# Convolution of the short channel chunk on GpSimd for two of four batches, and all stores of projection parts on SyncE's queue

## What is computed

```python
# mixer: depthwise convolution over time (7 taps), pointwise step, ReLU, pairwise maximum, 2-D DFT
h = conv_general_dilated(h, w_dw, padding='SAME', feature_group_count=192) + b_dw
h = einsum('od,bds->bos', w_pw, h) + b_pw
h = reduce_window(relu(h), -inf, max, (1, 1, 2), (1, 1, 2), 'VALID')
y = real(fft2(transpose(h)));  h = layernorm(y) * gamma + beta
# linear attention with a Taylor feature map, 12 heads of 16, causal
h = h + attention(layernorm(h))
# mixture of 8 experts, one per token, plus features of a tridiagonal resolvent
h = h + ffn(layernorm(h))
```

## Time and profile before

| what | value |
|---|---|
| timed runs | 428.26, 429.86, 433.29 us; median 429.86 |
| profiled execution | 426.79 us, its span 425.0 us |
| mean granted TensorE clock | 0.933 of full |
| TensorE matmul busy | 379.0 us, 89% of the span |
| VectorE busy | 281.1 us, 66% |
| ScalarE busy | 160.5 us, 38% |
| GpSimd busy | 103.0 us, 24% |
| DMA | 47.94 MB, mean 113 GB/s |

### The profile page before, as it was taken

One profiled execution on the slowest core, in us unless ns is written; L12 is line 12 of the kernel. 1 busy time (PEld: TensorE's weight loads), 2 busy tenths in 40 slices (PEclk: granted clock), 3 DMA queues, 4 the chain that ended last, 5 costly groups with the idle time before them and its releaser, 6 DMA issues.

```text
span 425.0 us, 7812 instructions
## 1 busy us (share of the span) xinstructions
PE 379.0 (89%) x2658; PEld 255.4 (60%) x2659; DVE 281.1 (66%) x901; ACT 160.5 (38%) x321; POOL 103.0 (24%) x154
## 2 busy tenths in 40 slices
PE   8999899799998998989998899995899999997273
PEld 4476547133673364723677228894899999996252
DVE  4589734899688995986433853664446656657783
ACT  1001131595317843187531781471243443441000
POOL 2000030151303612045300260310543443421000
PEclk9999899699999999999995799997899999999656
DMA  8664049400685015810279705310411112112504
GB/s 266 194 197 149 0 123 258 126 3 2 191 217 149 2 38 155 217 52 2 68 209 291 333 20 202 129 35 9 164 43 56 45 53 56 43 40 54 169 1 148
DMA packets 26900, 47.94 MB, mean 113 GB/s; under 512 B 11044, under 2 KB 21860, under 8 KB 25332
## 3 DMA queue, kind: packets, MB, share of 16 engines
q1 hardware_dynamic: 21412, 32.73, 25.0%
q10 hardware_dynamic: 2288, 7.15, 6.4%
q0 software_dynamic: 3168, 7.65, 6.2%
HBM read 36.84 MB, written 10.68 MB: 112 GB/s over the span
## 4 chain that ended last, share of the span: by engine, by line
PE 57%; DVE 24%; DMA 6%; issue 5%; ACT 4%; POOL 2%; DVEq 1%; SPq 0%; ACTq 0%; POOLq 0%
PE att L1664 10%; PE ring L1650 8%; PE ring L1654 5%; PE att L1527 4%; PE ring L1515 4%; ACT probs L674 3%; DMA w1b<-q_parts 3%; DVE wide L824 2%; PE att L1490 2%; POOL probs L603 2%; PE att L1581 2%; PE ring L1395 1%; PE ring L1361 1%; DVE stats L833 1%; PE ring L1400 1%
## 5 line engine op out<-in xcount | busy, mean ns | idle before, releaser
L674 ACT ACTIVATE probs<-ring,ones 128x1024 f32<-128x1024 f32 (+2 forms) x72 | 66.3, 970 | 15.9 <-PE ring L1515 14.5
L603 POOL TENSOR_SCALAR_AFFINE_SELECT probs<-probs 128x256 f32<-128x256 f32 (+1 forms) x72 | 40.7, 569 | 111.6 <-ACT probs L674 111.4
L1664 PE MATMUL att<-w,probs 128*128 x276 | 50.6, 335 | 3.3 <-DVE probs L1148 3.3
L1664 PEld LDWEIGHTS att<-w,probs 128*128 128x128 f32 x276 | 45.8, 195 | 4.2 <-issue 4.1
L1515 PE MATMUL ring<-w1b 128*128 128x512 bf16 (+3 forms) x192 | 40.6, 324 | 6.5 <-ACT probs L674 3.6
L824 DVE SCALAR_TENSOR_TENSOR wide<-w,wdw,wide 128x512 f32<-128x512 f32 x60 | 44.1, 779 | 0.8
L1527 PE MATMUL att<-probs,va 128*32 128x512 f32 (+3 forms) x384 | 39.8, 454 | 2.4 <-POOL probs L603 1.8
L629 POOL DMA_INDIRECT ffn_by_token<-probs,target_i x23 | 23.1, 1002 | 52.6 <-DVE probs L1154 44.7
L1515 PEld LDWEIGHTS ring<-w1b 128*128 128x128 bf16 x192 | 13.1, 101 | 37.8 <-ACT probs L674 26.5
L774 ACT ACTIVATE probs<-ring,q_area 128x128 f32<-128x128 f32 x72 | 19.9, 375 | 38.1 <-DVE k_area L1127 13.5
L619 POOL DMA_INDIRECT probs<-x_by_token,source_i x23 | 22.6, 984 | 41.4 <-issue 16.7
(11 more groups left out here) (369 smaller groups left out, 713.7 us busy)
## 6 DMA issues: line engine op xcount, KB each, us to landing
w1b<-k_parts ACTq DMA_DIRECT2D x16, 384.0 KB, 9.8
w1b<-q_parts SPq DMA_DIRECT2D x16, 384.0 KB, 9.1
w<-in_w SPq DMA_DIRECT2D x1, 4608.0 KB
w1a<-in_w1a SPq DMA_DIRECT2D x1, 3072.0 KB, 10.3
w<-in_x SPq DMA_DIRECT2D x4, 512.0 KB, 3.5
w<-in_x SPq DMA_DIRECT2D x8, 256.0 KB, 5.0
q_parts<-q_area SPq DMA_DIRECT2D x12, 128.0 KB, 2.6
k_parts<-k_area POOLq DMA_DIRECT2D x12, 128.0 KB, 2.6
```

What stands on the lines that cost most here:

```text
L603: nc.gpsimd.affine_select(diag, diag, [[0, len(UNITS[n][1])], [1, P]], ALU.is_ge, minus_one, base=0, channel_multiplier=-1).then_inc(p_rea ...
L674: nc.scalar.activation(squares(n), bank[:, :, 0:N - P * j], ACT.Square, bias=ones[:, 0:1], scale=0.25).then_inc(sq_done, 1)
L1664: last = nc.tensor.matmul(att[2][:, 0:D], hT[slot][:, c, :], w2[:, bass.ds((e * HC + c) * D, D)], start=(c == 0), stop=(c == HC - 1))
```

## The change

For the third and fourth batch GpSimd computes `conv_s`. The chain has one instruction for the first tap and two for each of the others, a multiply into a scratch tensor (`short_terms`, two of them in turn, in a free part of w2) and an addition, each waiting for the one ahead (`short_tap`). It stands in GpSimd's `project(b)`, between the selects of two attentions. `pointwise(2)` and `pointwise(3)` wait for it (`short_conv_done`) ahead of the short chunk's matmul, and SyncE's load of the fourth batch's input waits for the third's. VectorE's chain for the short chunk is taken out. GpSimd's stores go to SyncE, which now issues twelve a batch, each part as it is ready.

```diff
@@ -157,6 +157,8 @@
         at += 4 * P
         even_s, odd_s = (w2[:, at + P * i:at + P * i + P] for i in range(2))
         at += 2 * P
+        short_terms = [w2[:, at + N * i:at + N * i + N] for i in range(2)]
+        at += 2 * N
         assert at <= E * HC * D
 
         def of_parity(ap, h):
@@ -345,6 +347,7 @@
 
         zeroed, idle_zeroed = sem("buffers_zeroed"), sem("idle_operand_zeroed")
         conv_done = sem("conv_done")
+        short_tap, short_conv_done = sem("short_tap_done"), sem("short_conv_done")
         taps_ready, tap_sums_done, tap_sums_copied = sem("taps_ready"), sem("tap_sums_done"), sem("tap_sums_copied")
         pw_done = sem("pointwise_done")
         pool_done = sem("pooled_done")
@@ -457,17 +460,6 @@
                 src = dram_[0:2].rearrange("i d h n -> d i (h n)")
             eng.dma_start(dst.rearrange("p h n -> p (h n)"), src).then_inc(s_stack, 16)
 
-        def store_parts(eng, b, h, parts, ready):
-
-            if b > 0:
-                eng.wait_ge(s_stack, 16 * STACK_LOADS * b)
-            for i in range(PARTS):
-                rows = part_dram[h][i].rearrange("d h n -> (d h) n")
-                eng.wait_ge(ready[i], b + 1)
-                eng.dma_start(rows[0:P, :], parts[i]).then_inc(s_part_out[h], 16)
-                eng.wait_ge((s1_ready, s2_ready, s3_ready)[i], b + 1)
-                eng.dma_start(rows[P:D, :], s_parts[i][rows_of(h), :]).then_inc(s_part_out[h], 16)
-
         def store_out(eng, odd):
 
             for i in range(2):
@@ -486,6 +478,8 @@
                 if b > 0:
                     sp.wait_ge(tap_sums_done, min(b, 2))
                     sp.wait_ge(conv_done, 2 * b)
+                    if b > 2:
+                        sp.wait_ge(short_conv_done, b - 2)
                 sp.dma_start(xin[:, 0, HALO:HALO + S], t["x"][b, 0:P, :]).then_inc(s_x, 16)
                 for h in range(2):
                     first = HALO - 2 * h
@@ -504,7 +498,17 @@
 
             def project(b):
 
-                store_parts(sp, b, 0, q_parts, (q1_ready, q2_ready, q3_ready))
+                if b > 0:
+                    sp.wait_ge(s_stack, 16 * STACK_LOADS * b)
+                for i in range(PARTS):
+                    rows = [d[i].rearrange("d h n -> (d h) n") for d in part_dram]
+                    sp.wait_ge((q1_ready, q2_ready, q3_ready)[i], b + 1)
+                    sp.dma_start(rows[0][0:P, :], q_parts[i]).then_inc(s_part_out[0], 16)
+                    sp.wait_ge((k1_ready, k2_ready, k3_ready)[i], b + 1)
+                    sp.dma_start(rows[1][0:P, :], k_parts[i]).then_inc(s_part_out[1], 16)
+                    sp.wait_ge((s1_ready, s2_ready, s3_ready)[i], b + 1)
+                    for h in range(2):
+                        sp.dma_start(rows[h][P:D, :], s_parts[i][rows_of(h), :]).then_inc(s_part_out[h], 16)
                 sp.wait_ge(s_part_out[0], 16 * 2 * PARTS * (b + 1))
                 if b > 0:
                     sp.wait_ge(s_done, NU * b)
@@ -586,8 +590,28 @@
             def front(b):
                 pass
 
+            taps_of = Steps(pool, short_tap)
+
+            def convolve_short(b):
+
+                pool.wait_ge(s_x, 48 * (b + 1))
+                pool.wait_ge(pw_done, 2 * b)
+                for tap in range(TAPS):
+                    src = of_parity(xin[:, 1, tap:tap + S], 0)
+                    w = wdw[:, 1, tap:tap + 1]
+                    if tap == 0:
+                        taps_of.then(nc.gpsimd.tensor_scalar(in_pairs(conv_s), src, w, vec2[:, 0, 1:2], ALU.mult, ALU.add))
+                        continue
+                    term = in_pairs(short_terms[tap % 2])
+                    taps_of.then(nc.gpsimd.tensor_scalar(term, src, w, None, ALU.mult))
+                    last = nc.gpsimd.tensor_tensor(in_pairs(conv_s), in_pairs(conv_s), term, ALU.add)
+                    if tap < TAPS - 1:
+                        taps_of.then(last)
+                last.then_inc(short_conv_done, 1)
+
             def project(b):
-                store_parts(pool, b, 1, k_parts, (k1_ready, k2_ready, k3_ready))
+                if 0 < b < B - 1:
+                    convolve_short(b + 1)
 
             def attend(b):
                 if b == B - 1:
@@ -810,8 +834,6 @@
                     dve.wait_ge(pw_done, 2 * b)
                 long = lambda h: (xin[:, 0, :], conv[:, h, :], h, 0)
                 chains = [long(h) for h in halves]
-                if b >= 2 and 0 in halves:
-                    chains.append((xin[:, 1, :], conv_s, 0, 1))
                 for tap in some:
                     for src, dst, h, c in chains:
                         dst = in_pairs(dst)
@@ -1361,6 +1383,8 @@
                     nc.tensor.matmul(ring[0][:, h, :], wpw[:, 0, 0:P], conv[:, h, :], start=True, stop=False)
                 if b < 2:
                     pe.wait_ge(tap_sums_copied, b + 1)
+                else:
+                    pe.wait_ge(short_conv_done, b - 1)
                 for h in range(2):
                     last = nc.tensor.matmul(ring[0][:, h, :], wpw[rows_of(h), 1, 0:P], conv_s[rows_of(h), :],
                                             start=False, stop=True)
```

## The result

| | before | after |
|---|---|---|
| runs timed side by side, median | 429.06 us (427.32 to 433.29, 4 runs) | 433.81 us (430.70 to 436.19, 4 runs) |
| ratio, with its 95% interval | | 1.0118 [1.0068, 1.0167] |
| profiled execution, its span | 426.79, 425.0 us | 434.59, 432.8 us |
| VectorE, GpSimd busy | 281.1, 103.0 us | 279.8, 131.9 us |

The kernel is slower by 4.8 us between the medians, where +3.8 was forecast. The total came out; what it was made of did not.

A forecast was written before the change was run, and what follows sets the result against it. It took the first batch's stores and loads, and VectorE's convolution ahead of the fourth batch's pointwise step, as bound. 1.4 (fourth batch) + 0.4 (third) + 2.0 (stores) = +3.8 us on 429.86 gave 433.7 us, range 427.5 to 440.

The forecast's parts named there:

- Part 4: SyncE's stores in the first batch: k's stores delay the loads the first scores await, +2.0 us (1.0 to 2.4).
- Part 1: Fourth batch ahead of q's split: VectorE loses seven steps, 4.0 us less; gain at most 2.9 us; third batch nothing.
- Part 2: Short chunk's convolution, third and fourth batch: GpSimd's thirteen steps take 12.1 us (9.5 to 13.3), hidden in both.
- GpSimd becomes the bound: Rival, chance 0.18: third and fourth batch, GpSimd's chain, 21 us held, makes TensorE wait at L1365; 439 us.
- Part 3: Third and fourth batch: GpSimd's reads hold VectorE's steps with two SBUF inputs; +0.4 us third, +1.4 us fourth.
- three quarters: Share of VectorE's steps held beside GpSimd's chain: 3.9 us ahead of the fourth batch's split, 1.3 us in it.
- The relief stays: Rival, chance 0.27: reads meet less often or additions are short; fourth batch gains 1 to 2.9 us; 429.5 us.
- the stores cost nothing: Rival, chance 0.05: first batch's last load lands as early as today, held to the DMA engines' common rate; 431.7 us.
- The clock falls: Rival, chance 0.08: 3 us or more idle in the fourth batch halves TensorE's clock behind it; +3 us, 437 us.

The follow-up runs named there:

- the stores alone: Kernel before with SyncE issuing k's stores as well, the convolution left on VectorE: 429.77 us, ratio 1.0042 [1.0002, 1.0082].
- left out: Kernel before without the short chunk's convolution in the third and fourth batch, computed by nobody: 423.47 us, ratio 0.9927.
- writes only: Kernel after with thirteen GpSimd memsets in place of its thirteen convolution steps, short chunk's convolution not computed: 435.54 us, ratio 1.0167.
- the convolution alone: Kernel after, with GpSimd again storing k's parts in the first and fourth batch: 431.5 us, ratio 1.0071 [1.0031, 1.0111].
- four taps: Kernel after with GpSimd's chain ended after four of seven taps, the other three left out: 426.97 us, ratio 0.9997.
- only fourth: Two-operation multiply, GpSimd convolving for the fourth batch alone, k's stores on SyncE only in that one batch: 429.87 us, ratio 1.0078.
- both repairs: Kernel after with two-operation multiplies and k's stores on GpSimd's queue in the first and fourth batch: 431.3 us, ratio 1.0045.
- other forms: Kernel after with GpSimd's multiply adding 0.0 in the third batch and multiplying two tensors in the fourth: 433.04 us, ratio 1.0121.

## Why the total was right and the sum was not

The prediction named TensorE idle at L1365 until GpSimd's last addition as a sign that would make it wrong. That sign stands in the profile after, in both batches. That the number came out in spite of it is luck, in two parts: the median of the kernel before moved from 429.86 to 429.06 us with a fourth execution, and the pieces found in the profile add up to 1.5 us more than the medians show.

**Part 4, the stores: right within what can be told.** Forecast +2.0 (1.0 to 2.4), measured +1.7 in the profile and +1.8 (0.1 to 3.5) by the run with the stores alone, but only some 0.6 us between the means of all profiles with either queue. The last store of q's parts went out 61.85 - 56.29 = 5.6 us behind the first, where the prediction's pacing gave 5.9; the profile of before could tell this, since SyncE's own pace stood in the earlier trace rows. What the prediction had too small is how much of it comes back: the last store landed 2.06 us behind its issue, not 3.34, and the last load mostly took less time.

**Part 1, the relief: right.** 2.9 us forecast, 3.0 in the stretch and 3.1 (1.4 to 4.8) in the time when the steps were left out.

**Part 2, GpSimd's chain: this step failed.** "A multiply with one input I price like a select, 0.63 us" was wrong by a factor of 2.5: 1.60 us free. The addition was 1.26, not 1.07. With that, thirteen steps are 1.23 + 6 x 1.60 + 6 x 1.26 + 12 x 0.09 between them = 19.5 us, measured 21.1 and 22.1 with what GpSimd is held. "By itself GpSimd's chain is hidden in both" fell with it: the room was 18 us in the third batch. That is the rival *GpSimd becomes the bound*, with its 21 us and its +3 in the third batch (its +4 in the fourth did not come); I had given it 0.18, because both its prices lay "above the upper bounds from the selects". Those bounds were none: a select and a multiply share an engine and a shape, and nothing else that a row had shown. With the form that has a second operation, 0.73 us, the price of 0.63 would have been nearly right.
The Trainium skill, GPSIMD Engine Reference, 4.1 (Engine selection), calls one-input work on this engine roughly line-rate; the 1.60 us against 1.26 us for an addition of two tensors contradict that for the form without a second operation. The Trainium skill's figure in 3.1 (Elementwise), by which an addition was estimated at 1.12 us, was 0.14 us short.

**Part 3, the holding: the mechanism right, the size bound to a wrong term.** Time of VectorE's six and four taps ahead of the fourth batch's split, by what GpSimd did beside them:

| beside it | six | four | sum |
|---|---|---|---|
| nothing (left out), or writes only | 4.98 | 3.11 | 8.1 |
| multiply 1.60, addition 1.26 (after; the convolution alone and four taps within 0.02) | 5.79 | 4.69 | 10.5 |
| multiply 0.73, addition 1.26 (only fourth, both repairs) | 6.70 | 5.58 | 12.3 |
| multiply of two tensors (other forms) | 6.98 | 6.21 | 13.2 |

The steps of two of these rows, the kernel after and *only the fourth batch*:

```profile
151.41 5.79 DVE L846 SCALAR_TENSOR_TENSOR wide<-w,wdw,wide 128x512 f32<-128x512 f32 x6
...
158.65 4.69 DVE L846 SCALAR_TENSOR_TENSOR wide<-w,wdw,wide 128x512 f32<-128x512 f32 x4
```

```profile
146.58 6.70 DVE L874 SCALAR_TENSOR_TENSOR wide<-w,wdw,wide 128x512 f32<-128x512 f32 x6
...
154.19 5.58 DVE L874 SCALAR_TENSOR_TENSOR wide<-w,wdw,wide 128x512 f32<-128x512 f32 x4
```

The forecast was 3.9 us of holding up to the split and 1.3 in it, for a multiply of 0.63 us. With 0.73 us there were 4.2 us in the ten taps and 0.2 in the first tap of the second half, and 1.2 in the split. For the chain of the change it was less, 2.4 us in the ten taps, 0.75 in the first tap and 0.4 in the split, though GpSimd's steps were longer. So the "three quarters" holds for the steps that I had priced and for no others. That shorter steps of GpSimd meet VectorE's more often fits the table; whether the long multiply also reads in only a part of its time, no run tells. Wherever both engines read, more than half of the fourth batch's relief was gone, or all of it.
The memsets show that GpSimd's writes don't hold these taps. The Trainium skill, SBUF — State Buffer, Who interferes with whom, has the rule that a VectorE instruction with two SBUF inputs collides with a GpSimd instruction that reads SBUF and not with one that only writes; this case's runs agree with both halves of it (10.5 to 13.2 us against 8.1). The L950, one input in PSUM, stayed at 0.67 to 0.68 us in the fourth batch beside GpSimd's reads, as Part 3 had it.

**The sum.** Forecast: 2.0 stores, 0.4 third batch, 1.4 fourth. Measured: 1.8, 3.2, 1.3. The fourth batch's 1.3 is of another make than forecast, and so agrees by luck: TensorE waits 1.08 us for the divisions, less than before, and then 1.54 us for GpSimd. The third batch's +3.2 is the missing price of the multiply. These are 6.3 us, and the medians lie 4.8 apart (the ratio's interval allows 2.9 to 7.2); the 1.5 us between can't be assigned to a place, and are within what single pieces of the profile scatter.

**The other rivals.** *The relief stays* and *the stores cost nothing* are both spoken against by the runs with one part each, the first clearly (1.0071, from 1.0031), the second only just (1.0042, from 1.0002). Of the second a part is true: the last load goes out 1.2 us later every time, but about half of that comes back by the time the scores start. *The clock falls* did not happen at the new waits, but the mechanism exists: 1.55 us of idle time left the granted clock at 1.00, while it was at 0.50 behind the 2.8 us of the two kernels with the shorter multiply, the 3.5 us of the memsets and the 3.9 us of the multiply of two tensors. It cost 0.8 to 1.3 us of the fourth batch's stretch in three of these kernels, on top of what VectorE's holding cost them.

**A faster version?** None. The ratios of both repairs and of the four taps reach down to 1, but the four taps leave three out. In the kernels that compute everything, shortening GpSimd's chain took away TensorE's wait for GpSimd and gave back a longer one for VectorE, and with it some time at half the clock. What would avoid both, GpSimd's work placed where VectorE reads PSUM or nothing, was not tried.

## What to carry to other kernels

Price an instruction on GpSimd by its exact form, number of operations included, and where no row shows it, take no neighbour's duration as a bound: give the case in which it is too long its full weight. Work handed from VectorE to GpSimd beside it is full relief only if VectorE doesn't read two tensors in SBUF while GpSimd reads there; and making GpSimd's steps shorter can make VectorE slower. When a total agrees with a forecast, look at each term before believing the reasons: here a term short by 2.8 us passed unseen in a difference that was off by only 1.0, and in a median that was met to 0.1.

## What was not expected of the hardware

- A tensor_scalar on GpSimd over 128 x 512 f32 takes 1.60 us with one operation and 0.72 us with two, the second an addition of zero (0.86 us when the addend too is one per partition). It is the larger of the surprises, and its cause is open.
- VectorE's taps were held least by the GpSimd chain with the longest steps: 10.5 us for the ten taps in each of three kernels with 1.60 us multiplies, 12.3 us in both kernels with the 0.73 us form, 8.1 us beside memsets.
- The start of the first split moved by 4 us between executions of kernels that are alike up to there. The part behind the fourth batch's short chunk took between 254.3 and 261.5 us. Either is as large as the whole effect, so single profiles give stretches and not totals, and each part's time needs the median of several executions.
